# Layer norm merged into the opening of three streamed attentions, keys stacked through DRAM, the softmax sums' last tiles added on PE

## The chip, the cores and the metric

One NeuronCore of one Trainium2 chip. The metric is the device time of one execution in microseconds, lower is better. It is the whole four-layer model in one launch; the change touches the attention parts of layers 1, 2 and 3.

## The reference, cut to what matters

The input `x` is [2, 512, 512] (batch, sequence, features), the context [2, 1024, 512]. Four layers follow each other; each has an attention to the context and a feed-forward part, gated and added to `x`. The attentions of layers 1 to 3 have 16 heads of 32 features. All of them are, but for the differences named below, layer 3's, in float32:

```python
        Q = query @ Wq.T + bq
        K = key_value @ Wk.T + bk
        V = key_value @ Wv.T + bv
        Q = Q.reshape(B, S, NUM_HEADS, HEAD_DIM).transpose(0, 2, 1, 3)
        K = K.reshape(B, T, NUM_HEADS, HEAD_DIM).transpose(0, 2, 1, 3)
        V = V.reshape(B, T, NUM_HEADS, HEAD_DIM).transpose(0, 2, 1, 3)
        scale = 1.0 / np.sqrt(HEAD_DIM).astype(np.float32)
        scores = jnp.einsum('bhsd,bhtd->bhst', Q, K) * scale
        attn = jax.nn.softmax(scores, axis=-1)
        ctx = jnp.einsum('bhst,bhtd->bhsd', attn, V)
        ctx = ctx.transpose(0, 2, 1, 3).reshape(B, S, D_MODEL)
        return ctx @ Wo.T + bo
```

`query` is `_layernorm(x)`, `key_value` the context; layer 3's result is added as `x + jnp.tanh(g_xattn[3]) * ...`.

Layer 1 clips the scores to ±50, masks keys, and clips again. Layer 2 rounds the query and `Wq` to int8 steps per row before the query product (`_qdq`), and its output and the output weights likewise.

## The kernel before

**Products.** Every float32 product of the projections is made of three products of a high and a low part (`TERMS`), so each operand is first split: ACT copies the high part, DVE (or POOL, for Wq) subtracts it to get the low one. The context and the key and value weights are already split in DRAM (`ctx_parts`, `kv_parts`).

**Norm.** `norm_block` takes ACT's square root of the variance (line 250), lets DVE write the normed tiles (in layer 2 with the int8 rounding, lines 2242 to 2247), lets PE turn each of the 8 token tiles (line 235), and splits them into `x_parts`, which lie in the memory of the key stack. It also issues the first loads of the attention, splits Wq, and ends with a barrier of all engines. Then `streamed_attention_block` begins.

**Opening.** PE makes the queries of batch 0 (`("Q", 0, f)`, f being one of 4 feature groups of 4 heads), the keys of set 0 (`("K", 0, 0)` and `("K", 0, 1)`, in the changed list `K00` and `K01`, one for each half of the 1024 keys), the values, the queries of batch 1, and last the keys of set 1. In layers 2 and 3 the row maxima of set 0 are computed between these. Every query and key tile goes into one of 3 stage buffers. Queries are stored from there to DRAM (line 1454) and come back stacked in three copies for the four heads (line 1463). Keys are stacked by 12 DMAs of 64 KB from the stage buffer straight into `k_stack` (line 1475).

**The main loop.** There are 8 sets (feature group × batch), each of 32 units `u` (8 key tiles × 4 heads). In a unit PE computes one tile of scores (line 1603) and ACT its exponential (line 1708), and in layers 2 and 3 PE also computes one row-maximum product for the next set (line 1581), of which DVE takes the maximum (line 1794). These maxima are turned (transposed by PE) and *folded* by two small DMAs into the query stack (line 1482) as two more rows of the product, so that scores come out less their maximum; the first score of a set waits for its fold. In layer 1 DVE clips the scores instead (line 1806). Spread over the units (`CHUNK_AT`) are pieces of the keys of set n+2 (line 1553) and of the values of the next pair (line 1565). At u = 2, 10, 18, 26 PE multiplies two key tiles of probabilities by the values (line 1617). POOL adds the 8 probability tiles of a set into `total` (line 1760), seven adds per set; in set n+1 at `SUMS_AT`, u = 7, PE multiplies `total` by ones (line 1634) to get the softmax sums of set n, and at u = 8 to 11 (`INVERT_AT`) DVE takes reciprocals of a quarter each (line 1814). Sets in `SUMMED` (7, and in layer 1 also 6) don't use POOL: PE multiplies each tile by ones. ACT copies the product out (`COPY_AT`), POOL multiplies it by the reciprocals.

**Order.** Every engine's program is written out by hand in this order, and each engine runs its own in order. SP issues nearly all DMAs on one queue: among the key stacks it reloads the context with batch 1's half in set 1 (line 1312), reloads key weights (line 1315), value weights, and folds. The banks for products rotate over two, the order of use being `bank_order()`. A buffer is written again when the semaphores of its readers have come.

## Time and profile before

| what | us |
|---|---|
| median of 3 runs | 3204.24 (3200.37 to 3206.77) |
| the profiled execution's own time | 3191.67 |
| its span in the trace | 3190.0 |
| mean granted TensorE clock in it | 0.907 of full speed |
| PE busy | 2631.5 (82% of the span) |
| the three main loops (layers 1, 2, 3) | 321.3, 321.2, 317.2 |

The time of one core's whole launch is the metric; the page and the trace describe the one execution that was profiled. A stretch of the program is read in this order: how long it is, how much of it PE is busy, at which clock, and what ended PE's idle time in it. A loop is cut into its sets at the first score (line 1603) of each set. Layer 1's loop runs from 633.9 to 955.2, layer 2's from 1692.2 to 2013.4, layer 3's from 2385.8 to 2703.0 us.

### The profile page before, as it was taken

To read this page: it belongs to the slowest core of one execution; us is meant where nothing else is said; L and a number is where in the kernel's file an instruction comes from. 1 tells how busy PE (TensorE), PEld (TensorE's weight loads), DVE (VectorE), ACT (ScalarE), POOL (GpSimd) and SP (SyncE) were. 2 spreads that over 40 slices of the span, in tenths; PEclk is the share of its full clock that TensorE was granted. 3 is DMA by queue.
4 is the path that set the end of the run, shared out by engine and by line. 5 is a ranking of instruction groups with operands and counts; after the bars stand their busy time and mean duration, and the time that the engine had idled before them with its cause. 6 is when DMAs were issued, how large, how long until landed. Compare 5 with 4: busy or idle time off the path is not lost. (4 is left out here: it accounts for less than half of the span.)

```text
span 3190.0 us, 36367 instructions
## 1 busy us (share of the span) xinstructions
PE 2631.5 (82%) x11319; PEld 1675.3 (53%) x11319; DVE 1757.7 (55%) x3231; ACT 1197.2 (38%) x2550; POOL 1009.1 (32%) x450
## 2 busy tenths in 40 slices
PE   7798799778776459999968898738788897789898
PEld 3455487644423246656555564326565563477565
DVE  2444576356655889989365675422256673544321
ACT  1111222256552588878013455211124454222111
POOL 2111000078814100010014798023216795122122
PEclk9898899888888679999979998869999999899999
DMA  9653111634300010010053431063363430111822
GB/s 319 214 184 128 46 67 46 210 111 123 78 21 30 0 53 27 33 47 27 13 165 100 131 93 50 0 251 69 75 211 100 115 85 27 54 57 49 276 56 45
DMA packets 125501, 302.09 MB, mean 95 GB/s; under 512 B 23968, under 2 KB 27040, under 8 KB 120480
## 3 DMA queue, kind: packets, MB, share of 16 engines
q1 hardware_dynamic: 104672, 243.85, 24.0%
q0 software_dynamic: 12864, 29.06, 3.9%
q10 hardware_dynamic: 7808, 27.27, 2.5%
q8 instruction: 77, 1.26, 0.2%
q14 instruction: 80, 0.66, 0.1%
...
## 5 line engine op out<-in xcount | busy, mean ns | idle before, releaser
L1760 POOL TENSOR_TENSOR L_attn_total<-L_attn_total,L_attn_probs 128x2048 f32<-128x2048 f32 x120 | 552.8, 4607 | 79.1 <-ACT L_attn_probs L1708 68.7
L1794 DVE TENSOR_REDUCE L_attn_row_max<-L_attn_rows_ps 128x1 f32<-128x512 f32 x512 | 339.2, 685 | 184.2 <-PE L_attn_rows_ps L1581 179.0
L1708 ACT ACTIVATE L_attn_probs<-L_attn_s_ps 128x512 f32<-128x512 f32 x512 | 291.4, 602 | 326.8 <-PE L_attn_s_ps L1603 319.0
L516 PE MATMUL L_ffn_hidden<-L_ffn_x_high,L_ffn_up_high 128*128 128x512 f32 x688 | 296.6, 431 | 100.8 <-DVE L_ffn_routes L432 53.7
L1603 PE MATMUL L_attn_s_ps<-L_attn_q_stack,L_attn_k_stack 98*128 98x512 f32 (+1 forms) x768 | 318.2, 440 | 41.7 <-DMA L_attn_q_stack<-L_attn_top_parts 20.6
L398 ACT ACTIVATE L_ffn_sums<-sims 128x128 f32<-128x128 f32 x1024 | 315.8, 389 | 47.0 <-DVE L_ffn_routes L418 26.7
L516 PE MATMUL L_ffn_hidden<-L_ffn_x_low,L_ffn_up_high 128*128 128x512 f32 x688 | 273.6, 398 | 0.0
L1603 PEld LDWEIGHTS L_attn_s_ps<-L_attn_q_stack,L_attn_k_stack 98*128 98x128 f32 (+1 forms) x768 | 148.2, 198 | 188.7 <-issue 78.0
L1708 ACT ACTIVATE L_attn_probs<-L_attn_s_ps,keep_mask 128x512 f32<-128x512 f32 x256 | 182.2, 781 | 130.4 <-DVE L_attn_s_ps L1806 129.9
L537 PE MATMUL L_ffn_y<-L_ffn_down_in,L_ffn_h 128*128 128x512 f32 x512 | 229.1, 593 | 0.4 <-DVE L_ffn_h L644 0.4
L1581 PE MATMUL L_attn_rows_ps<-L_attn_k_stack,L_attn_q_stack 96*128 96x512 f32 x512 | 217.0, 432 | 8.8 <-DVE L_attn_row_max L1794 6.3
L1806 DVE TENSOR_SCALAR L_attn_s_ps<-L_attn_s_ps 128x512 f32<-128x512 f32 x256 | 162.9, 691 | 103.8 <-PE L_attn_s_ps L1603 102.1
L516 PEld LDWEIGHTS L_ffn_hidden<-L_ffn_x_high,L_ffn_up_high 128*128 128x128 f32 x688 | 132.7, 193 | 151.9 <-issue 81.2
L380 POOL TENSOR_TENSOR L_ffn_up_low<-L_ffn_up_in,L_ffn_up_high 128x512 fp32r<-128x512 f32 (+1 forms) x30 | 66.6, 2224 | 456.2 <-ACT L_ffn_up_high L374 456.2
L1617 PE MATMUL L_attn_o_ps<-L_attn_probs,L_attn_values 128*32 128x512 f32 x1536 | 199.6, 628 | 5.0 <-ACT L_attn_probs L1708 4.7
L1553 PE MATMUL L_attn_product_ps<-L_attn_ctx,L_attn_wk 128*128 128x512 f32 x576 | 170.1, 417 | 32.6 <-DMA L_attn_wk<-L_attn_kv_parts 29.2
L516 PE MATMUL L_ffn_hidden<-L_ffn_x_high,L_ffn_up_low 128*128 128x512 f32 x432 | 173.0, 400 | 0.0
L1565 PEld LDWEIGHTS L_attn_product_ps<-L_attn_wv,L_attn_ctx 128*128 128x128 f32 x1152 | 162.6, 193 | 19.0 <-issue 8.0
L1565 PE MATMUL L_attn_product_ps<-L_attn_wv,L_attn_ctx 128*128 128x256 f32 x1152 | 165.4, 284 | 7.7 <-DMA L_attn_wv<-L_attn_kv_parts 7.4
L155 POOL TENSOR_TENSOR L_attn_wq_parts<-L_attn_wq_raw,L_attn_wq_parts 128x512 fp32r<-128x512 f32 x12 | 15.6, 1323 | 435.8 <-ACT L_attn_wq_parts L259 435.8
L516 PEld LDWEIGHTS L_ffn_hidden<-L_ffn_x_low,L_ffn_up_high 128*128 128x128 f32 x688 | 133.1, 193 | 36.7 <-issue 10.8
L1553 PEld LDWEIGHTS L_attn_product_ps<-L_attn_ctx,L_attn_wk 128*128 128x128 f32 x576 | 115.5, 202 | 60.4 <-issue 30.0
...
## 6 DMA issues: line engine op xcount, KB each, us to landing
...
L_attn_abs_in<-in_L_ffn_w SPq DMA_DIRECT2D x12, 1024.0 KB, 11.1
...
L_attn_wk<-L_attn_kv_parts SPq DMA_DIRECT2D x24, 512.0 KB, 4.3
L_attn_wv<-L_attn_kv_parts SPq DMA_DIRECT2D x24, 512.0 KB, 8.9
q_parts<-L_attn_stage SPq DMA_DIRECT2D x24, 512.0 KB, 4.5
```

The costliest lines, as they stand in the source:

```text
L398: last = nc.scalar.activation(sums[:, h, a * NK:(a + 1) * NK], sims[:, t, h, KEY_ROWS:KEY_ROWS + NK], ACT.Identity, bias=sims[:, t, h, bas ...
L516: last = nc.tensor.matmul(hidden_ps[0:m, b, side, :], w[:, i, e0:e0 + m], x_parts[xp][:, i, h * HALF:(h + 1) * HALF], start=(q == 0), stop ...
L537: last = nc.tensor.matmul(y_ps[:, t % YB, :], h_parts[hp][0:m, s, c, t * P:(t + 1) * P], down_parts[wp][0:m, s, c, :], start=(q == 0), sto ...
L1553: last = nc.tensor.matmul(to, wk[:, w, c * P:(c + 1) * P], ctx[:, i, x, c, :], start=(c == 0 and (w, x) == TERMS[0]), stop=(c == DC - 1 an ...
L1565: last = nc.tensor.matmul(to[:, c // 2 * PAIR * P:(c // 2 + 1) * PAIR * P], ctx[:, i, x, d, at:at + P], wv[:, half, w, d % 2 * PAIR * P:(d ...
L1581: nc.tensor.matmul(rows_ps[:, r % R_SLOTS, :], q_stack[0:FOLD, n % Q_SLOTS, h, q * P:(q + 1) * P], k_stack[0:FOLD, n % 2, h, i * HALF:(i + ...
L1603: nc.tensor.matmul(s_ps[:, v % S_SLOTS, :], k_stack[0:depth, n % 2, h, kt * P:(kt + 1) * P], q_stack[0:depth, n % Q_SLOTS, h, :], start=Tr ...
L1617: last = nc.tensor.matmul(o_ps[HD * h:HD * (h + 1), :], values[:, n // PAIR % V_SLOTS, kt, at:at + HD], probs[:, g % P_SLOTS, h, :], start ...
L1708: nc.scalar.activation(probs[:, g % P_SLOTS, h, :], s_ps[:, v % S_SLOTS, :], ACT.Exp, **kinds).then_inc(exp_done, 1)
L1760: nc.gpsimd.tensor_tensor(total[:], first, probs[:, g % P_SLOTS], ALU.add).then_inc(added, 1)
L1794: nc.vector.tensor_reduce(row_max[:, hq, i:i + 1], rows_ps[:, r % R_SLOTS, :], AX_X, ALU.max, negate=True).then_inc(max_done, 1)
L1806: nc.vector.tensor_scalar(scores, scores, BOUND / SCALE, -BOUND / SCALE, ALU.min, ALU.max).then_inc(clipped, 1)
```

## The change

1. **Norm in the opening.** The separate norm stage and its barrier go for layers 1 to 3. Its steps join the attention's block: each X (turn a token tile and split it) and W (split a feature group of Wq) stands at a place in a list, `OPENING`, with the K, V and Q items. The rows of set 0's maxima ride on the last 6 items ahead of T (the turn), 8 rows of set 1 on the two after it.
2. **First loads** come as biases bq and bk, key weights, first context half, bv, Wq, second context half, value weights (before: Wq, first context half, the three biases, weights, second half). ACT waits for all three biases ahead of its square root.
3. **Keys through DRAM.** Each key tile is stored whole (512 KB, line 1491 of the changed kernel) and stacked by 3 DMAs of 256 KB (line 1510), in place of 12 of 64 KB.
4. **Batch 1's context** is loaded from ACT's queue at units 14 and 26 of set 1, no longer from SP's.
5. **Sums.** POOL leaves out the last tiles of a set (`DIRECT`: 1 in layers 2 and 3, 2 in layer 1, 3 in set 6); PE multiplies them by ones itself and adds them to the product. Only set 7 is summed wholly on PE. The sums of set n stand directly behind the last value product of set n (u = 2 of set n+1), and the reciprocals at u = 4 to 7.
6. Buffers are laid over each other (`x_parts` over `probs`, `wq_parts` over the query stack and `total`), and the output bank is part of the score banks' tensor.

```diff
     def first_loads(self, env, sp):
         io = env.io
-        sp.dma_start(self.wq_raw[:], io["wq"].rearrange("f p n -> p f n")).then_inc(self.wq_loaded, 16)
-        self.load_context(env, sp, 0, 0)
         for to, n in ((self.bq, "bq"), (self.bk, "bk")):
             sp.dma_start(to[:], io[n]).then_inc(self.biases_loaded, 16)
+        self.load_key_weights(env, sp, 0)
+        self.load_context(env, sp, 0, 0)
         sp.dma_start(self.bv[:], io["bv"].partition_broadcast(P)).then_inc(self.biases_loaded, 16)
-        self.load_key_weights(env, sp, 0)
+        sp.dma_start(self.wq_raw[:], io["wq"].rearrange("f p n -> p f n")).then_inc(self.wq_loaded, 16)
+        self.load_context(env, sp, 0, 1)
         self.load_value_weights(env, sp, 0)
-        self.load_context(env, sp, 0, 1)
...
-    SUMMED = range(SETS - 1 if less_max_rows else SETS - 2, SETS)
+    SUMMED = range(SETS - 1, SETS)
+    DIRECT = {n: 3 if n == SETS - 2 else 1 if less_max_rows else 2 for n in range(SETS - 1)}
...
-    SUMS_AT, TURN_AT, COPY_AT, PV_AT, PV_EVERY = 7, 26, 5, 2, 8
+    TURN_AT, COPY_AT, PV_AT, PV_EVERY = 26, 3, 2, 8
...
-    INVERT_AT = {SUMS_AT + 1 + part: part for part in range(4)}
-    NORM_KT = (SUMS_AT + 6) // HG
+    INVERT_AT = {PV_AT + 2 + part: part for part in range(4)}
+    NORM_KT = 2
...
+    if quantised:
+        order = "K00 K01 X0 X1 V00 V01 X2 X3 W0 W1 Q00 V02 V03 X4 X5 W2 W3 K10 K11 X6 X7 Q01 Q02 Q03 Q10 Q11 T0 Q12 Q13"
+    else:
+        order = "X0 X1 K00 X2 X3 W0 W1 K01 X4 X5 W2 W3 V00 X6 X7 V01 Q00 K10 K11 V02 V03 Q01 Q02 Q03 Q10 Q11 T0 Q12 Q13"
...
                 def stack_keys(n, i):
-                    for h in range(HG):
-                        for r, part in enumerate((0, 1, 0)):
-                            sp.dma_start(k_stack[HD * r:HD * (r + 1), n % 2, h, i * HALF:(i + 1) * HALF].bitcast(F32),
-                                         stage[HD * h:HD * (h + 1), stage_of["K", n, i], part, :].bitcast(F32)).then_inc(
-                                             stacked[n % 2][i][h], 16)
+                    for r, part in enumerate((0, 1, 0)):
+                        sp.dma_start(k_stack[HD * r:HD * (r + 1), n % 2, :, i * HALF:(i + 1) * HALF].bitcast(F32),
+                                     env.k_parts[n, i, :, part, :].rearrange("(h d) k -> d h k", d=HD).bitcast(F32)).then_inc(
+                                         stacked[n % 2][i], 16)
...
                 act.wait_ge(parts.biases_loaded, 48)
+                if not taken_before:
+                    act.wait_ge(var_done, TILES)
+                nc.scalar.activation(sd[:], meanvar[:, :, 1], ACT.Sqrt, bias=env.eps_ln[:]).then_inc(sd_done, 1)
...
+                        if n == FG - AHEAD - 1 and u in (14, 26):
+                            act.wait_ge(product_done, place["K", FG - 1, u // 26] + 1)
+                            parts.load_context(env, nc.scalar, 1, u // 26)
```

How instructions stand before and after, at three places. In the names, `s_ps` are scores, `rows_ps` the row-maximum products, `product_ps` the banks for projections and sums, `o_ps` the output of the value product (in the changed kernel printed as `s_ps`, of which it is a part).

**PE, layer 2, early in a set (u = 2 to 7).** Before, from the value product at u = 2 to the sums at u = 7:

```order
L1617 MATMUL L2_attn_o_ps<-L2_attn_probs,L2_attn_values 32x512 x8
L1603 MATMUL L2_attn_s_ps<-L2_attn_q_stack,L2_attn_k_stack 128x512
L1581 MATMUL L2_attn_rows_ps<-L2_attn_k_stack,L2_attn_q_stack 128x512
L1565 MATMUL L2_attn_product_ps<-L2_attn_wv,L2_attn_ctx 128x256 x6
L1603 MATMUL L2_attn_s_ps<-L2_attn_q_stack,L2_attn_k_stack 128x512
L1581 MATMUL L2_attn_rows_ps<-L2_attn_k_stack,L2_attn_q_stack 128x512
L1565 MATMUL L2_attn_product_ps<-L2_attn_wv,L2_attn_ctx 128x256 x6
L1603 MATMUL L2_attn_s_ps<-L2_attn_q_stack,L2_attn_k_stack 128x512
L1581 MATMUL L2_attn_rows_ps<-L2_attn_k_stack,L2_attn_q_stack 128x512
L1603 MATMUL L2_attn_s_ps<-L2_attn_q_stack,L2_attn_k_stack 128x512
L1581 MATMUL L2_attn_rows_ps<-L2_attn_k_stack,L2_attn_q_stack 128x512
L1634 MATMUL L2_attn_product_ps<-L2_attn_total,L2_attn_ones 32x512 x4
```

The same place in the changed kernel:

```order
L1637 MATMUL L2_attn_s_ps<-L2_attn_q_stack,L2_attn_k_stack 128x512
L1616 MATMUL L2_attn_rows_ps<-L2_attn_k_stack,L2_attn_q_stack 128x512
L1651 MATMUL L2_attn_s_ps<-L2_attn_probs,L2_attn_values 32x512 x8
L1671 MATMUL L2_attn_product_ps<-L2_attn_total,L2_attn_ones 32x512 x4
L1671 MATMUL L2_attn_product_ps<-L2_attn_probs,L2_attn_ones 32x512 x4
L1637 MATMUL L2_attn_s_ps<-L2_attn_q_stack,L2_attn_k_stack 128x512
L1616 MATMUL L2_attn_rows_ps<-L2_attn_k_stack,L2_attn_q_stack 128x512
L1600 MATMUL L2_attn_product_ps<-L2_attn_wv,L2_attn_ctx 128x256 x6
L1637 MATMUL L2_attn_s_ps<-L2_attn_q_stack,L2_attn_k_stack 128x512
```

The sums stand four units earlier and are twice as many matmuls in ordinary sets of layers 2 and 3.

**DVE, layer 2, a set's reciprocals.** Before:

```order
L1794 TENSOR_REDUCE L2_attn_row_max<-L2_attn_rows_ps 128x1 x11
L1779 TENSOR_TENSOR L2_attn_values<-L2_attn_product_ps,L2_attn_bv 128x512
L1794 TENSOR_REDUCE L2_attn_row_max<-L2_attn_rows_ps 128x1 x3
L1814 RECIPROCAL L2_attn_inv<-L2_attn_product_ps 128x128
L1794 TENSOR_REDUCE L2_attn_row_max<-L2_attn_rows_ps 128x1
L1814 RECIPROCAL L2_attn_inv<-L2_attn_product_ps 128x128
L1794 TENSOR_REDUCE L2_attn_row_max<-L2_attn_rows_ps 128x1
L1814 RECIPROCAL L2_attn_inv<-L2_attn_product_ps 128x128
L1794 TENSOR_REDUCE L2_attn_row_max<-L2_attn_rows_ps 128x1
L1814 RECIPROCAL L2_attn_inv<-L2_attn_product_ps 128x128
```

Changed (the reciprocals write `spare`):

```order
L1851 TENSOR_REDUCE L2_attn_row_max<-L2_attn_rows_ps 128x1 x10
L1871 RECIPROCAL L2_attn_spare<-L2_attn_product_ps 128x128
L1851 TENSOR_REDUCE L2_attn_row_max<-L2_attn_rows_ps 128x1
L1836 TENSOR_TENSOR L2_attn_values<-L2_attn_product_ps,L2_attn_bv 128x512
L1871 RECIPROCAL L2_attn_spare<-L2_attn_product_ps 128x128
L1851 TENSOR_REDUCE L2_attn_row_max<-L2_attn_rows_ps 128x1
L1871 RECIPROCAL L2_attn_spare<-L2_attn_product_ps 128x128
L1851 TENSOR_REDUCE L2_attn_row_max<-L2_attn_rows_ps 128x1
L1871 RECIPROCAL L2_attn_spare<-L2_attn_product_ps 128x128
```

The reciprocals stood three maxima behind the bias add of the values (line 1779, now 1836) and now begin ahead of it; there is one maximum between two of them either way.

**SP, layer 2, the opening up to set 1's keys.** Before:

```order
L1454 DMA q_parts<-L2_attn_stage 128x1024 x3
L1475 DMA L2_attn_k_stack<-L2_attn_stage 32x512 x24
L1315 DMA L2_attn_wk<-L2_attn_kv_parts 128x1024
L1463 DMA L2_attn_q_stack<-q_parts 32x4x512 x3
L1319 DMA L2_attn_wv<-L2_attn_kv_parts 128x1024 x2
L1454 DMA q_parts<-L2_attn_stage 128x1024 x4
L1482 DMA L2_attn_q_stack<-L2_attn_top_parts 1x16x128 x2
L1475 DMA L2_attn_k_stack<-L2_attn_stage 32x512 x24
L1315 DMA L2_attn_wk<-L2_attn_kv_parts 128x1024
L1463 DMA L2_attn_q_stack<-q_parts 32x4x512 x3
L1475 DMA L2_attn_k_stack<-L2_attn_stage 32x512 x12
```

Changed:

```order
L1491 DMA q_parts<-L2_attn_stage 128x1024
L1510 DMA L2_attn_k_stack<-k_parts 32x4x512 x3
L1328 DMA L2_attn_wv<-L2_attn_kv_parts 128x1024 x2
L1491 DMA k_parts<-L2_attn_stage 128x1024
L1501 DMA L2_attn_q_stack<-q_parts 32x4x512 x3
L1491 DMA k_parts<-L2_attn_stage 128x1024
L1510 DMA L2_attn_k_stack<-k_parts 32x4x512 x3
L1324 DMA L2_attn_wk<-L2_attn_kv_parts 128x1024
L1491 DMA q_parts<-L2_attn_stage 128x1024
L1510 DMA L2_attn_k_stack<-k_parts 32x4x512 x3
L1491 DMA q_parts<-L2_attn_stage 128x1024
L1501 DMA L2_attn_q_stack<-q_parts 32x4x512 x3
```

A key tile is now one store and three reads. Set 0's query stack (the first row of line 1501) stands behind the store of `K10`, the keys of set 1.

## Rows read from the trace of the kernel before

**Rows 1.** Windows, layer 1: opening, set 0, sets 1–5, 6, 7.

The columns are: the stretch, its length in us, then busy us (x instructions) of PE, PEld, DVE, ACT, POOL, then the granted clock, the DMA share, GB/s.

```profile
580.60:633.90 53.30, 49.87 (x241) 41.82 (x242) 11.03 (x15) 7.57 (x11) 0.00 (x0) 0.88 0.70 228
633.90:674.60 40.70, 28.30 (x154) 18.28 (x152) 22.12 (x35) 23.27 (x33) 19.70 (x5) 0.82 0.37 95
674.60:877.10 202.50, 159.57 (x881) 95.62 (x881) 131.65 (x201) 122.82 (x176) 166.23 (x41) 0.87 0.38 105
...
877.10:919.30 42.20, 31.93 (x153) 10.79 (x153) 23.06 (x37) 22.76 (x34) 14.62 (x4) 0.76 0.15 40
919.30:955.20 35.90, 30.80 (x160) 10.69 (x160) 22.33 (x36) 21.83 (x33) 1.27 (x1) 0.86 0.00 1
```

**Rows 2.** Windows, layer 2 (opening, sets 0, 1, 2, 3–5, 6, 7), layer 3 (loop).

```profile
1632.60:1692.20 59.60, 57.30 (x273) 45.80 (x274) 31.63 (x49) 7.82 (x12) 7.02 (x2) 0.95 0.49 150
1692.20:1744.70 52.50, 40.68 (x194) 25.41 (x193) 28.84 (x46) 21.14 (x37) 25.02 (x6) 0.87 0.32 81
1744.70:1792.70 48.00, 36.98 (x211) 23.44 (x210) 28.37 (x44) 20.37 (x37) 40.81 (x10) 0.92 0.60 187
1792.70:1832.00 39.30, 39.21 (x210) 25.43 (x210) 26.65 (x41) 19.69 (x36) 25.13 (x7) 0.93 0.22 56
1832.00:1943.60 111.60, 110.57 (x629) 70.54 (x628) 82.45 (x127) 60.09 (x109) 101.16 (x25) 1.00 0.33 84
...
1943.60:1978.60 35.00, 30.38 (x130) 12.99 (x130) 20.21 (x32) 17.79 (x34) 30.98 (x8) 0.85 0.18 59
1978.60:2013.40 34.80, 27.68 (x152) 9.37 (x152) 3.39 (x4) 16.49 (x34) 12.05 (x4) 0.90 0.00 0
...
2385.80:2703.00 317.20, 283.08 (x1521) 166.03 (x1520) 189.99 (x291) 155.53 (x283) 235.00 (x56) 0.94 0.31 85
```

**Rows 3.** Waits of PE, layer 1's loop: us in total, times, longest.

```profile
PE L_attn_product_ps L1634 <- POOL L_attn_total L1760: 24.8, 4, 7.1
PE L_attn_product_ps L1553 <- DMA L_attn_wk<-L_attn_kv_parts: 10.7, 1, 10.7
```

**Rows 4.** Waits of PE, layer 2's loop.

```profile
PE L_attn_s_ps L1603 <- DMA L_attn_q_stack<-L_attn_top_parts: 10.9, 1, 10.9
PE L_attn_product_ps L1553 <- DMA L_attn_wk<-L_attn_kv_parts: 9.3, 1, 9.3
```

**Rows 5.** The page's groups: POOL's adds, all three layers (busy, mean ns, idle before).

```profile
L1760 POOL TENSOR_TENSOR L_attn_total<-L_attn_total,L_attn_probs 128x2048 f32<-128x2048 f32 x120 | 552.8, 4607 | 79.1 <-ACT L_attn_probs L1708 68.7
```

**Rows 6.** Timeline of PE, sums (layers 1, 2), two row-maximum products: start, length, idle before.

```profile
850.02 1.94 PE L1634 MATMUL L_attn_product_ps<-L_attn_total,L_attn_ones 128*32 128x512 f32 x8 [7.04 <-POOL L_attn_total L1760]
...
1840.79 1.07 PE L1634 MATMUL L_attn_product_ps<-L_attn_total,L_attn_ones 128*32 128x512 f32 x8 [0.30 <-POOL L_attn_total L1760]
...
1842.12 0.40 PE L1581 MATMUL L_attn_rows_ps<-L_attn_k_stack,L_attn_q_stack 96*128 96x512 f32 x1
...
1842.59 0.40 PE L1581 MATMUL L_attn_rows_ps<-L_attn_k_stack,L_attn_q_stack 96*128 96x512 f32 x1
```

**Rows 7.** Timeline of DVE, layer 2, set 3: two reciprocals, one maximum between them.

```profile
1843.76 0.95 DVE L1814 RECIPROCAL L_attn_inv<-L_attn_product_ps 128x128 f32<-128x128 f32 x1
...
1845.17 0.94 DVE L1814 RECIPROCAL L_attn_inv<-L_attn_product_ps 128x128 f32<-128x128 f32 x1
```

**Rows 8.** Timeline of SP, layer 2, end of the opening: start, time issuing.

```profile
1691.13 15.09 SPq L1475 DMA_DIRECT2D L_attn_k_stack<-L_attn_stage  x24
```

**Rows 9.** Line 1482, the folds, all layers: from issue to landing.

```profile
DMA to landing us min/median/max: 1.8/1.8/13.3
```

**Rows 10.** Timeline of ACT: the square root of layer 1's norm.

```profile
568.72 0.30 ACT L250 ACTIVATE L_attn_sd<-tile_meanvar,eps_ln 128x8 f32<-128x8 f32 x1
```

**Rows 11.** Line 1328, bv (issued in layer 1 at 569.6): from issue to landing.

```profile
DMA to landing us min/median/max: 9.3/10.0/10.3
```

**Rows 12.** Timeline of PE, layer 2: the last of four pairs of turned tiles.

```profile
1628.58 1.97 PE L235 MATMUL L_attn_turned<-ident,L_attn_xn 128*128 128x128 f32 x8 [6.14 <-DVEq L213]
```

**Rows 13.** The page's DMA issues: stores of queries to DRAM (KB each, median us to landing).

```profile
q_parts<-L_attn_stage SPq DMA_DIRECT2D x24, 512.0 KB, 4.5
```

More of the change, by code:

```diff
@@ L1619, in pv @@
                     last.then_inc(pv_done, 1)
+                    if kt == KT - 1 and n not in SUMMED:
+                        sums(n)
                     if n in SUMMED:
@@ L1629, in sums @@
                 def sums(n):
-                    pe.wait_ge(added, (KT - 1) * (n + 1))
-                    pe.wait_ge(ones_made, 1)
+                    pe.wait_ge(added, adds_before[n + 1])
                     pe.wait_ge(product_free, place["S", n] - 1)
-                    for h in range(HG):
-                        last = nc.tensor.matmul(bank(("S", n))[HD * h:HD * (h + 1), :], ones[:], total[:, h, :],
-                                                start=True, stop=True)
-                    last.then_inc(product_done, 1)
@@ new lines, in sums, with turn_x @@
+                    for j, addend in enumerate(addends):
+                        for h in range(HG):
+                            last = nc.tensor.matmul(bank(("S", n))[HD * h:HD * (h + 1), :], ones[:], addend[:, h, :],
+                                                    start=(j == 0), stop=(j == len(addends) - 1))
+                    last.then_inc(product_done, 1)
+                def turn_x(t):
+                    pe.wait_ge(xn_done, t + 1)
+                    if t >= 4:
+                        pe.wait_ge(x_low, t - 3)
+                    for c in range(DC):
+                        last = nc.tensor.transpose(turned(t)[:, c, :], xn[:, t, c * P:(c + 1) * P], env.ident[:])
+                    last.then_inc(transposed, 1)
@@ L1651, in _ @@
+                pe.wait_ge(ones_made, 1)
+                for item in OPENING:
+                    if item[0] == "X":
+                        turn_x(item[1])
+                    elif item[0] == "T":
+                        turn(0)
+                    elif item[0] != "W":
+                        for c in range(DC):
+                            chunk(item, c)
+                            for of, r in opening_rows(item, c):
+                                row(of, r)
                 for n in range(SETS):
@@ L1652, in _ @@
                     for u in range(UNITS):
-                        if u == SUMS_AT and n and n - 1 not in SUMMED:
-                            sums(n - 1)
                         if less_max_rows and u == TURN_AT and n + 1 < SETS:
@@ L1675, in high_part @@
                     if at >= STAGES:
[L1676 to L1681 removed]
+                        stored(act, split_items[at - STAGES])
                     nc.scalar.activation(stage[:, stage_of[item], 0, :], bank(item), ACT.Identity, bias=bias_of(item)).then_inc(
@@ L1824, in _ @@
                         keep_values(*item[1:])
-                    else:
+                    elif item[0] != "W":
                         low_part(item)
-                for j in range(STEPS):
-                    for r in first_rows(j):
-                        maximum(0, r)
-                    if j % DC == DC - 1:
-                        item = WITH_ROWS[j // DC]
-                        if item[0] == "V":
-                            keep_values(*item[1:])
-                        else:
-                            low_part(item)
```

285 lines of the change are left out of this document (171 added, 114 removed).

## The prediction, as it was put on record

> **What bounds the kernel now.** I read the windows first, cut at the sets' first scores, then PE's waits in them, then single operations on PE, DVE and SP. The reader is to see that the loops fall in two kinds. In sets 3 to 5 of layer 2, PE is busy 110.57 of 111.60 us at full clock, 37.2 us a set [rows 2]; whatever is added to PE there is paid in full. Everywhere else PE idles: set 0 of layer 2 takes 52.5 us with 40.7 busy, set 1 takes 48.0 with 37.0 [rows 2], and one transfer ends most of each gap, 9.3 us for key weights and 10.9 us for the fold [rows 4]. Layer 1 has 10.7 us for key weights and 24.8 us in four waits for POOL's adds [rows 3]. POOL adds 7 tiles at 4.607 us [rows 5], 32.2 us a set, about as long as a set of layer 1 without its wait. PE's idle time there also goes with a lower clock: 0.87 in layer 1's sets 1 to 5 and 0.76 in its set 6, against 1.00 where it is never idle [rows 1, 2]. So waits can be removed, and so can what they do to the clock; against it stand PE's own work and the new openings.
>
> **An ordinary set of layers 2 and 3.** The direct tile adds one more 4-matmul pass of ones, which took 1.07 us for 8 records [rows 6]: +1.07. Second, the reciprocals now fall on u = 4 to 7. A reciprocal and the maximum behind it take 1.41 us (1845.17 − 1843.76) [rows 7], while PE passes a unit without a projection piece in 0.47 us (1842.59 − 1842.12) [rows 6]. PE may be only two row products ahead of the maxima, so it waits for DVE: four such pairs are 5.6 us, and with the bias add in between (0.68 us is a maximum's length, taken for it too) and the maximum at u = 8, about 7 us from the sums to the free row bank, against some 4 us of PE work. Before, the value product at u = 10 (16 records, about 1.9 us as are those of the sums at the lower clock [rows 6]) lay over the reciprocals of u = 8 to 11. Bounds: 0 if DVE's lead absorbs it, 4 × (1.41 − 0.47) = 3.8 if nothing does. I take 2.7, nearer the upper end, since POOL and ACT leave PE nothing else to do. An ordinary set becomes 37.2 + 1.07 + 2.7 = 40.9 us. The sums at u = 2 come sooner after POOL's last add, but POOL makes 6 adds (27.6 us) and not 7 (32.2) [rows 5]: no wait, 0.
>
> **Loop of layer 2.** Set 0: the key weights no longer stand behind 24 key stacks that take SP 15.1 us to issue [rows 8], so the 9.3 us go [rows 4]. Eight row products leave for the opening (8 × 0.47 = 3.8). The rest of PE's idle time, 52.5 − 40.7 − 9.3 = 2.5, mostly goes, and its clock of 0.87 rises: 52.5 → 34.7, −17.8. (Busy 40.7 × 0.87 is 35.4 at full clock, less 3.8 × 0.87 and plus 2.7 of the waits on DVE gives 34.8.) Set 1: the fold waited 10.9 us [rows 4] because 2 MB of context stood ahead of it in its queue; a fold's landing is 1.8 us at the median and 13.3 at worst [rows 9]. With the context on another queue I keep 1.5 us of waiting: 48.0 − 10.9 + 1.5 + 3.8 = 42.4, −5.6. Set 2: 39.3 → 40.9, +1.6 (the clock of 0.93 comes up, the two terms above come in). Sets 3 to 5: 3 × 3.7 = +11.1. Set 6: 35.0 → 32.5, −2.5; POOL had 8 adds in it and its sums were waited for [rows 2]. Set 7: three direct tiles in set 6's sums cost 3 × 1.07, the wait for POOL goes (clock 0.85 and 0.90 in these two, PE busy 58 of 70 us [rows 2]): 34.8 → 30.7, −4.1. Sum: −17.3 for the loop, which leaves 303.9. Layer 3's loop took 317.2 with the same instructions [rows 2]; at 303.9 too it gains 13.3.
>
> **Loop of layer 1.** Set 0: 40.7 less the 10.7 of the key weights [rows 3], less 2.5 for the clock (28.3 busy at 0.82, taken at 0.90): 27.5, −13.2. Sets 1 to 5: the 24.8 us for POOL go [rows 3], since POOL makes 5 adds (23.0 us) and no longer 7; two more passes of ones are 5 × 2 × 1.07 = +10.7; the clock gives back 159.6 × (1 − 0.87/0.90) = 5.3, of which I take 4.4: −18.5. Set 6: its tiles are no longer multiplied by ones as they come, 8 × 1.07 less two passes more for set 5's sums, −6.4, and half of a last wait on POOL of the kind in rows 3: −8.7 in all. Set 7: set 6's sums, four passes of 1.07, come here, less a rising clock: +2.5. Sum: −37.9. DVE's reciprocals cost nothing here, as no row maxima wait; ACT and the clips leave PE idle anyway (DVE 131.7 of 202.5 us [rows 1]).
>
> **Openings.** ACT now waits for bv ahead of the square root, which ran at 568.72 [rows 10]. bv was issued at 569.6 and took 9.3 to 10.3 us [rows 11] behind 3 MB; in the change it stands behind 2.5 MB. The norm starts some 8.5 us later. In exchange the barrier's idle time (PE's products started at 580.6, four us after the last turn), a stall for a free stage buffer and the order of queries and keys go. PE's work is the same 50 us [rows 1] and about 6 us of turns. Layer 1: 0. Layer 3: +6, since there 8 rows more are in the opening (+3 with their waits) and its opening ran at a higher clock already. Layer 2's norm is a chain on DVE: its four pairs kept PE waiting 6.1 us for the last [rows 12]. In the changed list these pairs stand behind the low parts of K00 and K01 in DVE's order, and K01 waits for the second half of the context, behind 5.75 MB of loads; Q00 then waits for the fourth low part, PE idle about 10 us; the rows of set 0 wait for Q00's stack, which on SP stands behind the store of K10, about 9 us. Against that stands what the norm cost alone, 31 us from 1601.6 to 1632.6 with PE nearly idle, of which some 22 are filled with products, less the 9 by which it starts later. My sum of this chain, item by item, is 107 us from the first load to the first score, against 96.4 before (1595.8 to 1692.2): +10. Bounds for it: −12 if the two waits are hidden, +16 if each is half longer.
>
> **Keys through DRAM.** A store and then a stack take longer than a direct stack. The nearest row is the store of a query tile of the same 512 KB, 4.5 us [rows 13]. Keys of set n+2 are stacked a whole set before they are read, so the cover is a set, some 37 us: 0. Without that cover it would cost the 4.5 us and a read.
> The Trainium skill, DMA: Bandwidth & Descriptors, section on the anatomy of one DMA on the SWDGE path, has 2.0 us plus bytes over 436 GB/s. An estimate by it: 3.2 us for the store and 3.8 us for three reads together. This queue is not of that path, and the trace's 4.5 us is longer. By the rule alone a key tile would be 7.0 us late where nothing covers it, and the sum would not change.
>
> **Sum**, against the profiled execution's 3191.7: layer 1 −37.9, layer 2 +10 −17.3, layer 3 +6 −13.3, together −52.5, so 3139. The profiled execution is 12.6 below the median, and before and after are compared as medians: 3204.2 − 52.5 = **3152 us**.
>
> **Rivals.**
> *Reciprocals hidden.* If the 2.7 us are not paid, in 12 sets (6 in each of two layers), 32 us more are gained, and better openings in layers 2 and 3 may add 10: 3110 to 3120. For it: DVE is busy only 82.5 of 111.6 us [rows 2]. Against it: two row banks are all the lead that there is.
> *The clock falls.* New idle time of PE at u = 3 to 10 of each ordinary set may bring its clock down, as in layer 1's sets (0.87 with PE busy 79%) [rows 1]. A set at 0.87 costs 37.2/0.87 − 37.2 = 5.6 us more; over 11 ordinary sets of layers 2 and 3 that is 61 us, and the result is 3213, slower than before. It decides from 52.5/11 = 4.8 us a set. For it: in set 2 of layer 2 the clock was 0.93 with PE busy 39.2 of 39.3 us [rows 2], so it can be low after one gap. Against it: gaps of 1 us before the last units of sets don't show it. At half that price it gives 3183.
> *Openings.* If bv's wait and the chain on DVE cost 10 us more in each layer, 3182.
> *POOL still late.* Sums at u = 2 leave POOL 5 units less. If its last add of layers 2 and 3 is late by 2 us in each of 12 sets, 3176. Its 27.6 us of 37.2 [rows 5, 2] speak against.
> *Folds.* A fold may still wait for context that ACT's queue loads. The Trainium skill, DMA: Bandwidth & Descriptors, section on queues, rings and completion order, says that an engine takes turns between its queues; by that the fold shares the engines for a while, and does not wait for the whole 2 MB. The nearest rows are the 1.8 and 13.3 us of rows 9. By the longer one set 1 keeps its 10.9 us in two layers: 3171.
>
> **Chances.** Around the forecast (gain 30 to 85 us): 0.55. More (reciprocals hidden): 0.12. Less, 6 to 30 us (openings, half the clock's price, POOL, folds): 0.18. Within 0.2%, 6.4 us, about what a measurement of this kernel can tell from no change: 0.05. Slower (the clock): 0.10. The range has to hold 8 in 10: from 3100, where hidden reciprocals lie inside, to 3192, where most of the smaller gains do; it leaves out the last 12 us of them, no change and slower. Faster 0.85, same 0.05, slower 0.10.
>
> **What would show it.** No wait for key weights in sets 0; a wait for the fold in set 1 of at most some 2 us; sums without POOL in layer 1, whose sets 1 to 5 take 184 us; in layers 2 and 3 PE idle about 2.7 us between u = 3 and 10 with DVE's maxima as the releaser, and sets of 40.9 us at a clock near 1.00; in layer 2's opening idle PE ahead of Q00 and ahead of the first row product. It is wrong if sets 3 to 5 keep 38.3 us (no reciprocal cost), if their clock is under 0.95, or if layer 2's first score comes over 20 us later or earlier against its first load than the 107 us above.

## The result, and the profile after

The changed kernel takes 3176.48 us at the median (3171.44 to 3183.25) against 3200.37 us before, timed beside it: a ratio of 0.9939 with the interval 0.9924 to 0.9954. It is faster by 0.6%, where 1.6% (52 us) was forecast: the medians differ by 23.9 us, and the ratio stands for 19.5. The profiled execution took 3171.77 us, its span is 3169.8 us, 20.2 less than before.

Where the time went, from the first load of each attention to its first score (opening) and from there to its last score (loop), in us:

| stretch | before | after | difference | forecast |
|---|---|---|---|---|
| layer 1, opening | 66.5 | 65.8 | −0.7 | 0 |
| layer 1, loop | 321.2 | 277.9 | −43.3 | −37.9 |
| layer 2, opening | 96.4 | 111.0 | +14.6 | +10 |
| layer 2, loop | 321.3 | 320.3 | −1.0 | −17.3 |
| layer 3, opening | 72.1 | 85.5 | +13.4 | +6 |
| layer 3, loop | 317.2 | 316.6 | −0.6 | −13.3 |
| all else | 1995.2 | 1992.7 | −2.5 | 0 |

The two loops of layers 2 and 3 are 29.0 us longer than forecast and the openings 11.3; layer 1's loop and all else are 7.9 us shorter. All else is code that the change leaves alone. What stands ahead of layer 1's first load was 5.7 us shorter in this execution, and in the profiles below its length varies from 561.7 to 571.2 us. For single mechanisms the stretches are therefore compared, not whole spans.

Windows of the changed kernel, layer 1: set 0, sets 1 to 5, 6, 7 (to be read beside [rows 1]), with the same columns:

```profile
627.50:656.10 28.60, 25.93 (x153) 16.73 (x151) 22.65 (x36) 23.72 (x34) 18.59 (x5) 1.00 0.53 167
656.10:838.00 181.90, 160.87 (x960) 95.72 (x961) 130.98 (x201) 121.39 (x176) 119.86 (x30) 0.95 0.50 141
838.00:870.00 32.00, 25.38 (x121) 7.91 (x121) 23.00 (x37) 22.69 (x34) 21.75 (x7) 0.89 0.34 84
870.00:905.50 35.50, 31.17 (x176) 10.40 (x176) 22.30 (x36) 22.14 (x33) 4.04 (x2) 0.90 0.01 1
```

PE has 79 more records in sets 1 to 5 than before and the sets take 20.6 us less: POOL is busy 120 and not 166 us, and the clock is 0.95 and not 0.87.

Layer 2: set 0, set 1, set 2, sets 3 to 5 (beside [rows 2]):

```profile
1657.80:1692.30 34.50, 33.79 (x187) 22.98 (x185) 24.70 (x39) 20.81 (x37) 24.19 (x6) 1.00 0.37 108
1692.30:1745.40 53.10, 40.43 (x218) 24.60 (x217) 28.31 (x44) 20.25 (x37) 31.93 (x8) 0.90 0.57 174
1745.40:1789.20 43.80, 41.94 (x217) 26.50 (x218) 26.73 (x41) 19.61 (x36) 24.82 (x7) 0.89 0.34 91
1789.20:1912.10 122.90, 117.31 (x653) 73.66 (x652) 82.58 (x127) 59.94 (x109) 86.24 (x22) 0.96 0.39 102
```

Set 0 (34.5, forecast 34.7) and an ordinary set (41.0, forecast 40.9) are as forecast. Set 1 is the surprise: 53.1 us, 5 more than before, where 42.4 stood in the sum; set 2 takes 2.9 more than its 40.9, at a clock of 0.89 and with PE idle for 1.9 us only. Sets 6 and 7 take 33.5 and 32.4 us, where 32.5 and 30.7 were forecast. In layer 3 set 1 takes 52.1 us, against 46.6 before.

PE's waits in layer 2's loop (us in total, times, longest), beside [rows 4]:

```profile
PE L_attn_rows_ps L1616 <- DVE L_attn_row_max L1851: 11.6, 15, 1.4
PE L_attn_s_ps L1637 <- DMA L_attn_q_stack<-L_attn_top_parts: 5.8, 1, 5.8
PE L_attn_rows_ps L1616 <- DMA L_attn_k_stack<-k_parts: 4.8, 1, 4.8
```

The wait for key weights is gone. In its place PE waits in set 1 for the stack of set 3's keys (4.8 us), of which the last units of the set compute the first row products, and then still for the fold (5.8 us). The timelines of ACT's and SP's DMA issues show the order:

```profile
1713.79 0.34 ACTq L1321 DMA_DIRECT2D L_attn_ctx<-ctx_parts  x1
```

```profile
1715.31 0.34 SPq L1491 DMA_DIRECT2D k_parts<-L_attn_stage  x1
1723.94 1.25 SPq L1510 DMA_DIRECT2D L_attn_k_stack<-k_parts  x3
```

The 2 MB of context are issued 1.5 us ahead of the 512 KB store. SP waits 8.6 us for that store and only then issues the stack. The second half goes the same way: its context is issued at 1734.0 us, its store at 1734.8 lands after 10.2 us, and the fold's two DMAs, issued right behind, after 7.7 and 9.1. From issue to landing all stores of the changed kernel (line 1491, keys and queries) took

```profile
DMA to landing us min/median/max: 2.6/3.0/12.6
```

so 3.0 us at the median; the store of set 4's keys at 1772.1, with no context load on the way, took 2.6.

PE's waits in the openings, layer 2 and then layer 3:

```profile
PE L_attn_product_ps L1588 <- DMA L_attn_ctx<-ctx_parts: 18.9, 2, 14.8
PE L_attn_rows_ps L1616 <- DMA L_attn_q_stack<-q_parts: 11.9, 1, 11.9
PE L_attn_product_ps L1579 <- DVE L_attn_x_parts L1921: 10.1, 1, 10.1
```

```profile
PE L_attn_s_ps L1680 <- DVE L_attn_heads L1887: 30.2, 1, 30.2
PE L_attn_rows_ps L1616 <- DMA L_attn_q_stack<-q_parts: 5.0, 1, 5.0
```

Layer 2 shows the two waits of the forecast, 10.1 us ahead of Q00 and 11.9 ahead of the first row product. In layer 3 the first turned tile comes 30.2 us after PE's last work, against 19.0 before: ACT's square root waits for bv. But it also waits 5.0 us for the query stack, which the forecast had in layer 2 only.

### The profile page after: what moved, and what is told of

Read it like the earlier page. It is cut to its first block and busy times, and to the rows that moved or that the text cites. A ratio compares the mean times of both kernels' runs of the same rounds, so it can differ in the third digit from the quotient of the medians.

```text
span 3169.8 us, 36099 instructions
## 1 busy us (share of the span) xinstructions
PE 2641.6 (83%) x11527; PEld 1677.5 (53%) x11527; DVE 1755.2 (55%) x3231; ACT 1193.7 (38%) x2550; POOL 884.4 (28%) x424
## 5 line engine op out<-in xcount | busy, mean ns | idle before, releaser
L1817 POOL TENSOR_TENSOR L_attn_total<-L_attn_total,L_attn_probs 128x2048 f32<-128x2048 f32 x93 | 426.2, 4583 | 77.7 <-ACT L_attn_probs L1748 69.5
L1616 PE MATMUL L_attn_rows_ps<-L_attn_k_stack,L_attn_q_stack 96*128 96x512 f32 x512 | 224.8, 442 | 54.2 <-DVE L_attn_row_max L1851 25.8
L1637 PEld LDWEIGHTS L_attn_s_ps<-L_attn_q_stack,L_attn_k_stack 98*128 98x128 f32 (+1 forms) x768 | 145.4, 193 | 158.9 <-ACT L_attn_probs L1748 66.5
L1651 PE MATMUL L_attn_s_ps<-L_attn_probs,L_attn_values 128*32 128x512 f32 x1536 | 200.7, 631 | 6.5 <-ACT L_attn_probs L1748 6.4
L1588 PE MATMUL L_attn_product_ps<-L_attn_ctx,L_attn_wk 128*128 128x512 f32 x576 | 174.0, 424 | 25.7 <-DMA L_attn_ctx<-ctx_parts 19.1
L1817 POOL TENSOR_TENSOR L_attn_total<-L_attn_probs 128x2048 f32<-128x2048 f32 x21 | 95.8, 4561 | 345.9 <-ACT L_attn_probs L1748 345.9
L1616 PEld LDWEIGHTS L_attn_rows_ps<-L_attn_k_stack,L_attn_q_stack 96*128 96x128 f32 x512 | 101.5, 198 | 117.0 <-DVE L_attn_row_max L1851 53.8
```

The source lines that it names most:

```text
L1588: last = nc.tensor.matmul(to, wk[:, w, c * P:(c + 1) * P], ctx[:, i, x, c, :], start=(c == 0 and (w, x) == TERMS[0]), stop=(c == DC - 1 an ...
L1616: nc.tensor.matmul(rows_ps[:, r % R_SLOTS, :], q_stack[0:FOLD, n % Q_SLOTS, h, q * P:(q + 1) * P], k_stack[0:FOLD, n % 2, h, i * HALF:(i + ...
L1637: nc.tensor.matmul(s_ps[:, v % S_SLOTS, :], k_stack[0:depth, n % 2, h, kt * P:(kt + 1) * P], q_stack[0:depth, n % Q_SLOTS, h, :], start=Tr ...
L1651: last = nc.tensor.matmul(o_ps[HD * h:HD * (h + 1), :], values[:, n // PAIR % V_SLOTS, kt, at:at + HD], probs[:, g % P_SLOTS, h, :], start ...
L1817: nc.gpsimd.tensor_tensor(total[:], first, probs[:, g % P_SLOTS], ALU.add).then_inc(added, 1)
```

## The experiments

Each kernel is the changed one with an edit. Ratios are against the kernel before, run beside it.

**The context later.** What holds up set 1?

```diff
-                        if n == FG - AHEAD - 1 and u in (14, 26):
-                            act.wait_ge(product_done, place["K", FG - 1, u // 26] + 1)
-                            parts.load_context(env, nc.scalar, 1, u // 26)
+                        if (n, u) in ((FG - AHEAD - 1, 20), (FG - AHEAD, 4)):
+                            half = n - (FG - AHEAD - 1)
+                            act.wait_ge(product_done, place["K", FG - 1, half] + 1)
+                            parts.load_context(env, nc.scalar, 1, half)
```

> The changed kernel with one edit: the first half of batch 1's context is issued from ACT's queue at unit 20 of set 1 (was 14), the second half at unit 4 of set 2 (was 26 of set 1). Theory A (the reload's packets share the DMA engines with the store and the stack of set 3's keys, and with the fold): set 1 of layers 2 and 3 falls from 53.1 and 52.1 us to 42 to 46 us, the 4.8 us wait of the row products for the key stack is gone, the fold waits under 3 us; 15 to 20 us for both layers. Rival B (keys are late because a store and a stack through DRAM take too long in themselves): the 4.8 us wait stays and set 1 keeps at least 50 us.

Ratio 0.9874 (0.9853 to 0.9894). Set 1 of layer 2, and its waits:

```profile
1702.64:1745.86 43.22, 38.24 (x218) 23.73 (x217) 28.42 (x44) 20.33 (x37) 31.35 (x8) 1.00 0.54 165
```

```profile
PE L_attn_s_ps L1637 <- DMA L_attn_q_stack<-L_attn_top_parts: 2.9, 1, 2.9
PE L_attn_rows_ps L1616 <- DVE L_attn_row_max L1852: 2.0, 3, 1.4
```

43.2 us in both layers; the key wait is gone, the fold waits 2.9. The loops are 9.7 and 7.0 us shorter than in the changed kernel, 16.7 in all, as theory A has it. Set 2 stayed at 43.9 us. PE waits for no transfer inside it, although the second half of the context is loaded in it; its clock is 0.89, behind the 2.9 us of waiting for the fold.

**No reload at all.**

```diff
-                            parts.load_context(env, nc.scalar, 1, u // 26)
+                            nc.scalar.dma_start(ctx[:, i, 0, 0, 0:16].bitcast(F32), env.ctx_parts[0, i, :, 0, 0, 0:16].bitcast(F32)).then_inc(
+                                parts.ctx_loaded[i], 16)
```

> The changed kernel without the reload: batch 1's half of the context is not read, two small transfers of 8 KB stand in its place, so the attentions of batch 1 use batch 0's keys and values. Theory A: set 1 of layers 2 and 3 takes 41 to 42.5 us, as an ordinary set does, and both waits are gone. Rival B: the row products still wait for the keys of set 3, 4 us or more.

```profile
1701.49:1742.05 40.56, 38.20 (x219) 23.77 (x218) 27.89 (x44) 20.31 (x37) 28.71 (x8) 1.00 0.45 125
```

Set 1 takes 40.6 and 40.2 us, set 2 40.2 and 40.9, and layer 2's loop 303.5 us. That set 1 is a little under the 41 to 42.5 expected changes nothing: both waits are gone. So the way through DRAM alone costs no wait; with the reload beside it the loop is 16.8 us longer, in layer 3 13.7. This kernel was timed once, so it has no interval; the stretches of the two layers agree.

**The reload on SP's queue again,** at the old places (8 lines moved to SP's program).

```diff
+                    if n == FG - AHEAD - 1:
+                        sp.wait_ge(product_done, place["K", FG - 1, 0] + 1)
+                        parts.load_context(env, sp, 1, 0)
```

> The changed kernel with batch 1's context issued from SP's queue again, at the places of the kernel before. If a queue of its own on ACT saves the fold nothing, because the engines are shared, set 1 of layers 2 and 3 stays at 51 to 54 us; if being in one queue is what costs, as the prediction had it, the fold waits 9 to 12 us and the set takes 55 us or more; if the other queue itself is the harm, it falls under 50 us.

Ratio 0.9922 (0.9906 to 0.9939). Set 1 of layer 2 takes 48.6 us, layer 3's 48.4:

```profile
PE L_attn_s_ps L1643 <- DMA L_attn_q_stack<-L_attn_top_parts: 7.9, 1, 7.9
```

There is no wait for the keys, as the context now stands behind their stack. The fold waits 7.9 us, 2.1 more than on ACT's queue. Moving the reload to a second queue bought the fold 2 us and lost the keys 5; the set is 4.5 us shorter without the move, by the third of the expected ways. But layer 3's whole loop is not shorter (316.6 us both ways, its set 2 taking 44.9 and not 42.9), and the ratio's interval overlaps that of the changed kernel, so for the whole kernel no gain is shown.

**Keys stacked directly,** by 12 DMAs from the stage buffer as before the change.

```diff
-                    for r, part in enumerate((0, 1, 0)):
-                        sp.dma_start(k_stack[HD * r:HD * (r + 1), n % 2, :, i * HALF:(i + 1) * HALF].bitcast(F32),
-                                     env.k_parts[n, i, :, part, :].rearrange("(h d) k -> d h k", d=HD).bitcast(F32)).then_inc(
+                    for h in range(HG):
+                        for r, part in enumerate((0, 1, 0)):
+                            sp.dma_start(k_stack[HD * r:HD * (r + 1), n % 2, h, i * HALF:(i + 1) * HALF].bitcast(F32),
+                                         stage[HD * h:HD * (h + 1), stage_of["K", n, i], part, :].bitcast(F32)).then_inc(
```

> The changed kernel with keys stacked as before the change, 12 DMAs of 64 KB from the stage buffer, no store to DRAM. Theory A (in set 1 the store of set 3's keys shares the engines with the context and SP waits for it before it can stack): without the store the keys of set 3 are there sooner, the row products wait under 2 us of 4.8, set 1 takes 47 to 51 us instead of 53.1 and 52.1. Other sets: within 0.3 us of 41.0 if the cover of a set's remainder is enough for either way. SP is busy issuing for 8.4 us per key tile, and if the folds wait for that, sets 2 to 6 are longer by that wait and the way through DRAM is worth having.

Ratio 0.9958 (0.9942 to 0.9975). Set 1 is 46.1 and 45.6 us, a little under the expected range, the key wait 0.4 us:

```profile
PE L_attn_s_ps L1645 <- DMA L_attn_q_stack<-L_attn_top_parts: 5.1, 1, 5.1
PE L_attn_rows_ps L1624 <- DVE L_attn_row_max L1859: 2.0, 3, 1.4
PE L_attn_rows_ps L1624 <- DMA L_attn_k_stack<-L_attn_stage: 0.4, 1, 0.4
```

Ordinary sets keep 41.0 us. But the openings grow, by 13.7, 6.7 and 4.3 us. SP's timeline in layer 1's opening points at the reason: a tile's 12 issues take about 8 us, and the stacks and stores of queries stand between and behind them. The first line is PE's longest wait after the first turn, for the low part of a product, which is written once a stage buffer is free:

```profile
PE L_attn_product_ps L1587 <- DVE L_attn_stage L1835: 9.2, 1, 9.2
```

```profile
596.52 8.16 SPq L1518 DMA_DIRECT2D L_attn_k_stack<-L_attn_stage  x12
604.79 1.49 SPq L1508 DMA_DIRECT2D L_attn_q_stack<-q_parts  x3
607.69 7.94 SPq L1518 DMA_DIRECT2D L_attn_k_stack<-L_attn_stage  x12
```

So the way through DRAM is worth 24.7 us in the new openings and costs 13.5 in the two sets with the reload; the direct way ends the wait for keys with the reload in place, and leaves the fold's.

**Reciprocals later.**

```diff
-    INVERT_AT = {PV_AT + 2 + part: part for part in range(4)}
+    INVERT_AT = {PV_AT + 6 + part: part for part in range(4)}
```

> The changed kernel with the reciprocals of the sums at units 8 to 11 (were 4 to 7), sums still at unit 2. If the reciprocals beside the row maxima are what an ordinary set of layers 2 and 3 pays beyond the added pass of ones, it falls from 41.0 to 38.0 to 38.6 us and the clock of sets 3 to 5 comes back to 1.00; 11 such sets give about 28 us. Rival: the place of the sums costs, or the probabilities held longer; then the set stays above 40 us.

Ratio 0.9831 (0.9809 to 0.9854). Sets 3 to 5 of layer 2:

```profile
1787.93:1903.28 115.35, 113.22 (x653) 71.41 (x652) 82.28 (x127) 59.99 (x109) 86.37 (x22) 1.00 0.42 109
```

38.4 us a set, 2.5 less, at full clock. That is 37.2 + 1.07 and 0.2. The loops of layers 2 and 3 are 16.1 and 10.7 us shorter. Layer 1's sets 3 to 5 gained too, 35.6 to 34.1 us, which I hadn't expected. There PE had waited in sets 1 to 5 for 6.5 us in five places for the bias add of the values (line 1836), which stood among the reciprocals, and this wait is 3.4 now. But in sets 3 to 5 PE's idle time fell by only 0.5 us a set (11.6 to 10.1 in all); the other 1.0 us is PE's work at a clock of 1.00 and not 0.97.

**Sums in layers 2 and 3 as before the change,** with the late reciprocals: seven adds on POOL (`DIRECT` 0 in sets 0 to 5), sums at u = 7.

```diff
-    DIRECT = {n: 3 if n == SETS - 2 else 1 if less_max_rows else 2 for n in range(SETS - 1)}
+    DIRECT = {n: 3 if n == SETS - 2 else 0 if less_max_rows else 2 for n in range(SETS - 1)}
+    SUMS_AT = 7
```

> The kernel with the reciprocals at units 8 to 11, and in layers 2 and 3 the sums of sets 0 to 5 as before the change: seven adds on POOL, sums at unit 7. An ordinary set there goes from 38.4 to 37.2 us, the 1.07 us of one pass of ones less and the length of before; if the longer chain on POOL is late again, it stays at 38 us or more with a wait on POOL. 10 sets give 10 to 14 us against the kernel with the late reciprocals.

Ratio 0.9804 (0.9778 to 0.9830). Sets 3 to 5 of layer 2:

```profile
1786.28:1897.18 110.90, 110.50 (x629) 70.53 (x628) 82.39 (x127) 59.99 (x109) 100.13 (x25) 1.00 0.42 113
```

37.0 us a set, the old length. The edit takes out the direct pass and puts the sums back to u = 7; together they are 1.5 us a set, and at least the 1.07 of the pass is paid where PE is the bound. What the place of the sums costs by itself no run shows. POOL, 100 us busy of 111, is still not late. The two loops are 4.2 and 6.8 us shorter than with the late reciprocals alone, 11.0 in all.

**The same in layer 1 only,** where the direct tiles should be the gain. This kernel was timed once.

> The kernel with the reciprocals at units 8 to 11, and in layer 1 the sums of sets 0 to 5 as before the change: seven adds on POOL, sums at unit 7. If the direct tiles are what freed layer 1 of its waits for POOL, its sets 2 to 5, 34.0 us in the kernel with the late reciprocals, go back to 40 to 41 us and sums wait 6 to 7 us for POOL in them; if the key weights and the transfers were what held them, they stay under 37 us.

Sets 1 to 5 with the old sums and, above them, PE's wait in them:

```profile
PE L_attn_product_ps L1673 <- POOL L_attn_total L1821: 24.5, 4, 6.9
```

```profile
661.70:859.38 197.68, 157.76 (x880) 94.35 (x881) 131.37 (x201) 122.18 (x176) 167.05 (x41) 0.88 0.46 129
```

197.7 us against 178.3 with the direct tiles (the single sets 38.7 to 39.7, a little under the 40 expected), and the wait and the clock of before, 24.5 us and 0.88 (24.8 and 0.87 in [rows 3, 1]). So these 19.4 us are the direct tiles' with the earlier sums; over the whole loop the two kernels differ by 26.5 us (300.5 and 274.0). The rest of layer 1's gain is the wait for key weights in set 0, which is gone here too.

**The norm ahead of the biases:** ACT's first wait for the biases is deleted.

```diff
-                act.wait_ge(parts.biases_loaded, 48)
                 if not taken_before:
```

> The changed kernel with ACT's wait for the three biases taken from ahead of its square root (it stays ahead of the first tile to which a bias is added). If the late bv holds up the openings of layers 1 and 3 as a whole, each first score comes 8 to 10 us sooner after its first load; if the loads of context and weights are what ends last, under 3 us. Layer 2: 3 to 9 us sooner, as its chain of quantising on DVE starts earlier but stands behind the first two key tiles after its first pair.

Ratio 0.9930 (0.9905 to 0.9955), no different from the changed kernel. The openings take 67.5, 112.0 and 89.2 us, so none of them is shorter; layer 3's is 3.7 us longer, at a clock of 0.83 where it was 0.85. PE in layer 1's opening:

```profile
PE L_attn_s_ps L1680 <- DVE L_attn_heads L1886: 12.0, 1, 12.0
PE L_attn_product_ps L1588 <- DMA L_attn_ctx<-ctx_parts: 9.6, 2, 5.2
```

The first tiles are turned 2.6 us after the first load, not 12.8, and PE then waits 9.6 us for the two halves of the context. In layer 3 PE's longest wait for a turned tile falls from 30.2 to 20.4 us, and the opening gains nothing by it. My step "the norm starts some 8.5 us later" came true (the square root runs 11.6 us after the first load, before 1.3) and had no price in this order of items: K01 can't start until the second half lands, 19.2 us after the first load in the changed kernel and 19.3 here.

**Another order of the openings** on top of that.

```diff
-        order = "X0 X1 K00 X2 X3 W0 W1 K01 X4 X5 W2 W3 V00 X6 X7 V01 Q00 K10 K11 V02 V03 Q01 Q02 Q03 Q10 Q11 T0 Q12 Q13"
+        order = "X0 X1 K00 X2 X3 W0 W1 Q00 X4 X5 W2 W3 X6 X7 K01 V00 V01 Q01 K10 K11 V02 V03 Q02 Q03 Q10 Q11 T0 Q12 Q13"
...
-        order = "K00 K01 X0 X1 V00 V01 X2 X3 W0 W1 Q00 V02 V03 X4 X5 W2 W3 K10 K11 X6 X7 Q01 Q02 Q03 Q10 Q11 T0 Q12 Q13"
+        order = "X0 X1 K00 X2 X3 W0 W1 K01 X4 X5 V00 W2 W3 V01 X6 X7 Q00 Q01 K10 K11 V02 V03 Q02 Q03 Q10 Q11 T0 Q12 Q13"
```

> The changed kernel with ACT's early wait for the biases gone and another order of the openings. Layers 1 and 3: all token tiles are turned and Q00 is made between K00 and K01, in the time in which the second half of the context is on its way. Layer 2: the same idea, X0 X1 first, so that DVE quantises the next pair before it waits for a key tile, and Q00 well ahead of the rows of set 0. Theory C (the openings are late because of where the items stand, K01 waiting for the context's second half about 20 us after the first load, in layer 2 Q00 for DVE's chain and the rows for Q00's stack behind K10's store): layer 2's opening falls from 111 us to 88 to 96 us, layer 3's from 85.5 to 76 to 81 us, layer 1's from 65.8 to 61 to 65 us. Rival D (the loads of 8 MB and the work of PE set the length): less than 3 us in each.

Ratio 0.9847 (0.9820 to 0.9874). Layer 2's opening falls by 19.1 us to 91.9, layer 3's by 4.5 to 81.0, layer 1's by 1.2: theory C in layer 2, barely in layer 3, and in layer 1 no more than rival D gives. Against the run above, which differs by the order alone, it is 20.1, 8.2 and 2.9 us. Windows of layer 2's opening, in the changed kernel and in this one:

```profile
1546.80:1657.80 111.00, 70.89 (x314) 55.99 (x315) 69.49 (x122) 15.72 (x27) 12.11 (x6) 0.78 0.56 178
```

```profile
1548.14:1640.04 91.90, 67.36 (x314) 54.34 (x314) 69.01 (x122) 15.90 (x27) 12.52 (x6) 0.85 0.68 215
```

The wait ahead of Q00 is gone, that for the query stack is 5.2 us and not 11.9. Layer 3's opening stays 9 us longer than before the change. What remains there isn't settled; the kernel before began with query products, for which only 1 MB had to be there, and no run tried that in the new block.

**All together:** the new openings, the context later, late reciprocals, old sums in layers 2 and 3.

> All edits together: norm ahead of the biases and the new orders of the openings, the context reload later, reciprocals at units 8 to 11, the old sums in layers 2 and 3. If the causes add up: against the changed kernel about 11 us from the context, 25 to 28 from the reciprocals, 12 from the old sums and 20 to 30 from the openings, so 3100 to 3115 us where the changed kernel has 3176; loops of layers 2 and 3 under 290 us.

3097.72 us (3088.19 to 3103.68), ratio 0.9683 (0.9662 to 0.9704): 3.2% faster than before, 2.5% faster than the changed kernel (3097.72 / 3176.48, two sets of runs). Its three loops:

```profile
631.60:903.68 272.08, 238.68 (x1409) 127.66 (x1407) 197.82 (x307) 189.77 (x274) 164.41 (x41) 0.96 0.43 121
1637.20:1926.46 289.26, 280.49 (x1536) 164.65 (x1534) 185.53 (x284) 155.19 (x283) 219.61 (x53) 0.97 0.38 109
2309.38:2598.38 289.00, 280.68 (x1536) 164.84 (x1534) 185.59 (x284) 155.16 (x283) 219.55 (x53) 0.97 0.38 109
```

In layers 2 and 3 PE is now busy 97% of the loop. The causes add up, with a time a little under the 3100 to 3115 us expected.

## Why the prediction was wrong

The direction was right, the size was not: 0.6% for a forecast of 1.6%.

*Right.* The bound of each kind of set, and most of their lengths: an ordinary set of layers 2 and 3, 40.9 forecast and 41.0 measured. Its cost of 3.8 us is the reciprocals' place (2.5 us go when they are later) and the direct pass with the place of the sums (1.5 more). PE and DVE in a set of layer 2 (1789.2 is its first score); the rows to compare are [rows 6, 7]:

```profile
1800.06 0.50 PE L1616 MATMUL L_attn_rows_ps<-L_attn_k_stack,L_attn_q_stack 96*128 96x512 f32 x1 [0.42 <-DVE L_attn_row_max L1851]
1802.15 0.47 PE L1616 MATMUL L_attn_rows_ps<-L_attn_k_stack,L_attn_q_stack 96*128 96x512 f32 x1 [1.36 <-DVE L_attn_row_max L1851]
```

```profile
1799.37 0.63 DVE L1851 TENSOR_REDUCE L_attn_row_max<-L_attn_rows_ps 128x1 f32<-128x512 f32 x1
1799.92 0.68 DVE L1836 TENSOR_TENSOR L_attn_values<-L_attn_product_ps,L_attn_bv 128x512 f32<-128x512 f32 x1
1800.51 0.95 DVE L1871 RECIPROCAL L_attn_spare<-L_attn_product_ps 128x128 f32<-128x128 f32 x1
```

PE's idle time there is 1.8 us (0.42 + 1.36), and not the 2.7 that I had as waiting. The rest is the clock, 0.96 in these sets and 1.00 before, and it falls right behind the second gap:

```profile
1803.20:1806.40 3.20, 3.20 (x12) 1.91 (x14) 2.35 (x4) 1.00 (x2) 1.72 (x1) 0.50 0.00 0
```

The rival that the clock falls came true for about a third of the term, not for 5.6 us a set. That idle time and clock together gave my 2.7 is luck in part: I had priced the wait too high and the clock at nothing.

*The step that failed: "Keys of set n+2 are stacked a whole set before they are read ... 0".* They are not. The first 8 row products of set n+2 stand at u = 24 to 31 of set n, as `JOIN_AT` and `EARLY_ROWS` in the code say; its first key tile is ready at u = 13 and can't be stacked before the scores of u = 15 have freed the place. The cover is 8 units, not 32. In ordinary sets a 3 us store and a 4.8 us stack fit in it. In set 1 the reload made the store take 8.6 us, and 4.8 us stuck out. This with the fold (5.8 us, for which 1.5 stood in the sum) and the clock, 0.90 and 0.89 in the two sets, are the 10.7 us of set 1 and 2.9 of set 2 in layer 2. With keys stacked directly 7.0 of the 10.7 are gone (46.1 us) and the fold's 3.7 are left; with the context later 9.9 are gone. Layer 3 is alike: its set 1 takes 52.1 us, and its loop misses the forecast by 12.7 us where layer 2's misses by 16.3. The other 2.7 us of layer 2 are in sets 6 and 7, which vary by 1 to 2 us between layers and runs. Without the reload the loop took 303.5 us, which is the forecast length, but in part by luck: sets 1 and 2 are 2.6 us under their forecasts and sets 6 and 7 are 2.0 over. I had seen the two parts of the change and priced each by itself, the store as if alone on the engines and the context as if its only neighbour were the fold.
The Trainium skill's rule that I cited (DMA: Bandwidth & Descriptors, queues, rings and completion order: the engines take turns between queues) agrees with the trace in that the fold is served while the context is on the way: it waited 5.8 us, against 7.9 with the reload back on SP's queue. What I drew from it, that the fold does not wait for the whole 2 MB, did not come out: its second DMA landed at 1745.4 us, 0.7 us after the context's half that was issued 2.3 us ahead of it on the other queue. The second queue moved the wait rather than ended it.

*Openings, mis-sized.* Layer 2: two waits were forecast at 10 and 9 us and measured at 10.1 and 11.9; +10 was +14.6. Layer 3: +6 was +13.4. Of this, the 5.0 us for the query stack stood in layer 2's account only, though the order there is the same: Q00's stack behind K10's store. And the late bv, to which I gave 8.5 us as a cause, was none by itself: with it removed, PE waits for the context instead, whose second half lands 19 us after the first load. What the order of the items is worth is shown: 19.1 us of layer 2's opening, 4.5 of layer 3's, 1.2 of layer 1's. Why layer 3's is still 8.9 us longer than before the change stays open.

*Layer 1, better than forecast,* 43.3 against 37.9: I had taken the clock to 0.90, it rose to 0.95 with the idle time gone. More of the 5.4 us is in sets 6 and 7, 32.0 and 35.5 us where 33.5 and 38.4 were forecast. That the reciprocals cost nothing there was wrong by about 1.5 us in each of sets 3 to 5.

*The range* (3100 to 3192) held the time, but in part by luck: a wait that two parts of the change make together was in none of the rivals. The rival of the fold at its full old price would have given a time 5 us off the measured one, for half of the right reason.
